# Decoder layer: who sums the norm's mean and variance in the first half, and where the residual stands

## The reference

```python
x = _layernorm(x + _L0_attn_ref(x, ...), axis=-1)
x = _layernorm(x + _L0_xattn_ref(ctx_2048, x, mask, mask, ...), axis=-1)
x = _layernorm(x + _L0_ffn_ref(x, ...), axis=-1)

def _layernorm(x, axis=-1, eps=1e-05):
    m = jnp.mean(x, axis=axis, keepdims=True)
    v = jnp.var(x, axis=axis, keepdims=True)
    return (x - m) / jnp.sqrt(v + eps)
```

## Time and profile before

| | us |
|---|---|
| median of 3 runs | 1878.28 |
| lowest, highest | 1867.21, 1881.26 |
| the profiled execution | 1870.93 |
| its span | 1869.1 |

### The profile page before, as it was taken

The page is one execution under the profiler, slowest core; times in us unless marked ns, Lnnn a source line. Parts: engine busy times, 40 slices in busy tenths (PEclk is TensorE's granted clock), DMA queues, the critical chain, the costliest instruction groups (busy, mean ns, idle before and its releaser), DMA issues. The chain is left out here.

```text
span 1869.1 us, 32453 instructions
## 1 busy us (share of the span) xinstructions
PE 1775.7 (95%) x12432; PEld 978.3 (52%) x12432; DVE 1374.0 (74%) x1466; ACT 770.5 (41%) x1208; POOL 566.8 (30%) x578
## 2 busy tenths in 40 slices
PE   7999999999999998978899999999999999999988
PEld 3665456545654564634545555455454554554543
DVE  2899999999999999957566577575675666657721
ACT  3323222222232222237657265373562744726522
POOL 3125865596559525600100302003011020030000
PEclk9999999999999999999999999999999999999999
DMA  9436346535653467556430613405205143051010
GB/s 217 128 74 136 97 124 153 130 79 137 148 123 85 118 143 184 156 147 201 103 74 2 142 46 74 113 1 130 57 14 134 40 106 81 1 137 28 13 34 23
DMA packets 295166, 183.86 MB, mean 98 GB/s; under 512 B 194015, under 2 KB 251359, under 8 KB 295038
## 3 DMA queue, kind: packets, MB, share of 16 engines
q1 hardware_dynamic: 287392, 178.50, 38.3%
q10 hardware_dynamic: 7646, 3.50, 1.0%
HBM read 94.82 MB, written 33.62 MB: 69 GB/s over the span
## 5 line engine op out<-in xcount | busy, mean ns | idle before, releaser
L1223 POOL TENSOR_TENSOR q<-q,x_hi 128x512 f16<-128x512 f32 x28 | 40.5, 1475 | 597.5 <-ACT x_hi L1571 597.5
L1251 PE MATMUL b_ff<-x2T_hi,w1T_hi 128*128 128x512 f16 x512 | 195.3, 381 | 2.3 <-DVE x2T_lo L1661 2.3
L1251 PE MATMUL b_ff<-x2T_lo,w1T_hi 128*128 128x512 f16 x512 | 195.3, 381 | 0.0
L1251 PE MATMUL b_ff<-x2T_hi,w1T_lo 128*128 128x512 f16 x512 | 195.1, 381 | 0.0
L1661 DVE TENSOR_TENSOR p_lo<-k,p_hi 128x1024 f16<-128x1024 f32 x128 | 161.3, 1260 | 37.4 <-ACT p_hi L1517 37.4
L1550 ACT ACTIVATE k<-b_st,mbias 128x512 f32<-128x512 f32 x256 | 161.9, 693 | 41.4 <-PE b_st L1318 37.9
L1711 DVE SCALAR_TENSOR_TENSOR top<-b_st,mleast,top 128x512 f16<-128x512 f32 x168 | 126.1, 751 | 51.5 <-PE b_st L1278 34.5
L825 DVE TENSOR_TENSOR prod<-q,k 128x4096 f32<-128x4096 f32 x32 | 143.0, 4469 | 20.7 <-ACT q L691 19.9
L607 PE MATMUL sm_b<-cT_hi,wsT_hi 128*128 128x256 f16 x512 | 141.1, 276 | 14.7 <-DMA cT_lo<-rows_lo 12.2
L457 POOL TENSOR_TENSOR rows_lo<-cn,rows_hi 128x512 f16<-128x512 f32 x64 | 131.4, 2061 | 61.0 <-ACT rows_hi L675 61.0
L571 PE MATMUL pj_b<-winT_hi,xT_hi 128*128 128x512 f16 x384 | 148.1, 386 | 0.9 <-DVE winT_lo L892 0.9
(11 more groups left out here) (287 smaller groups left out, 4314.1 us busy)
## 6 DMA issues: line engine op xcount, KB each, us to landing
cn<-in_ctx_dram SPq DMA_DIRECT2D x64, 256.0 KB, 3.3
k<-kT_scratch SPq DMA_DIRECT2D x24, 512.0 KB, 7.9
x<-in_x_dram SPq DMA_DIRECT2D x32, 256.0 KB, 3.1
x_scratch<-x SPq DMA_DIRECT2D x32, 256.0 KB, 2.3
q<-x_scratch SPq DMA_DIRECT2D x8, 1024.0 KB, 5.6
q<-x_scratch SPq DMA_DIRECT2D x32, 256.0 KB, 2.8
out_dram<-q SPq DMA_DIRECT2D x32, 256.0 KB, 3.3
xn<-in_x_dram SPq DMA_DIRECT2D x24, 256.0 KB, 2.9
```

What stands on the lines that cost most here:

```text
L1251: mm = pe.matmul(out, a, c, start=(start and n == 0), stop=end)
```

## The change

Three edits in `phase_a`.

- For tiles 0 to 28 (`SUMMED = 29`) VectorE stops after the residual sum. ACT gets `moments(n)`: one pass over the row that sums `-E**-1.5 * x` (into mean times `-E**-0.5`), and a second that squares `E**-0.5 * x + mv0` and sums it, which is the variance. Both write their 512 unused results into the bank `om_b[n % 2]`. They stand in ACT's order behind the copies of the projections and `normalize`, in the step in which VectorE has its residual.
- TensorE's output projection of tile n waits for `ln_mv` of tile n-2 instead of `om_used`, since ACT uses the bank until then.
- In the score steps VectorE has residual (and moments) between the products and the sums.

POOL's factors take a mean that is scaled: a product takes the place of the difference, four instructions as before.

```diff
+def layer_norm_factors_of_sums(pool, w, mv, vs, out, done, at):
+
+    pool.tensor_tensor(vs[:, :], mv[:, 1:2], w.consts[:, 1:2], ALU.add).then_inc(done, 1)
+    pool.wait_ge(done, at + 1)
+    pool.tensor_tensor(out[:, 0:1], vs[:, :], w.consts[:, 0:1], ALU.pow).then_inc(done, 1)
+    pool.wait_ge(done, at + 2)
+    pool.tensor_tensor(out[:, 2:3], mv[:, 0:1], out[:, 0:1], ALU.mult).then_inc(done, 1)
+    pool.wait_ge(done, at + 3)
+    pool.tensor_tensor(out[:, 1:2], w.consts[:, 5:6], out[:, 2:3], ALU.mult).then_inc(done, 1)
...
@@ TensorE, output_projection
                 if n >= 2:
-                    pe.wait_ge(s["om_used"], n - 1)
+                    pe.wait_ge(s["ln_mv"], n - 1)
...
@@ ScalarE
+            def moments(n):
+                i, unused = n % 3, om_b[n % 2][:, :]
+                act.wait_ge(s["om_used"], n + 1)
+                if n >= 3:
+                    act.wait_ge(s["ln_rstd"], 4 * n - 8)
+                act.activation(unused, x1[i][:, :], ACT.Identity, scale=-E ** -1.5,
+                               accum_out=mv[i][:, 0:1]).then_inc(s["ln_stats"], 1)
+                act.wait_ge(s["ln_stats"], n + 1)
+                act.activation(unused, x1[i][:, :], ACT.Square, bias=mv[i][:, 0:1], scale=E ** -0.5,
+                               accum_out=mv[i][:, 1:2]).then_inc(s["ln_mv"], 1)
...
                 for n in plan.tiles(g - 4):
                     normalize(n)
+                for n in plan.tiles(g - 3):
+                    if n < SUMMED:
+                        moments(n)
...
@@ VectorE, residual_and_moments
+                if n < SUMMED:
+                    return
                 dve.wait_ge(s["om_used"], n + 1)
+                dve.wait_ge(s["ln_mv"], n)
                 dve.bn_stats(stats[i][:, :], x1[i][:, :]).then_inc(s["ln_stats"], 1)
...
@@ VectorE, steps
                     score_products(b, t)
+                    for n in plan.tiles(g - 3):
+                        residual_and_moments(n)
                     for n in plan.quarters(g - 1):
                         stage_lo(n)
                     score_sums(b, t)
-                    for n in plan.tiles(g - 3):
-                        residual_and_moments(n)
```

## The result

| | before | after |
|---|---|---|
| median of 4 runs, us | 1877.2 | 1935.1 |
| lowest to highest, us | 1867.2 to 1881.3 | 1931.9 to 1939.6 |
| span of the profiled execution, us | 1869.1 | 1937.8 |
| mean granted clock over it | 0.987 | 0.975 |

The changed kernel is slower: ratio 1.033, 95% interval 1.030 to 1.035, some 58 us. The forecast was 1924 us within 1900 to 1948. Nearly all of it is the first half: the second begins at 819.9 us before and at 887.5 after.

The account below looks back on a forecast made before the run. TensorE and VectorE were taken to be full at once, so the effect on TensorE counts. Waits +50.4, `c1T` -7.7, `stage_lo` with its half clock -9.2, quarters -3.0, clock +20.4: +51 on 1874, given as 1924 us, range 1900 to 1948.

Parts of the forecast that it names:

- What bounds the kernel: From 60 to 810 us TensorE (718 of 750 us busy) and VectorE (707) are both full; relieving one hands on the bound.
- Where the wait falls, and how often: TensorE's output projection waits for ScalarE's moments of tile n-2 in 18 places, steps 16b+12 to 16b+17, b = 0, 1, 2.
- The price of a wait: Copy, normalize and two passes end 2.88 us behind the last p matmul's start; each wait 2.8 us, together +50.4 us.
- `c1T` never later than the moments: In these steps the new wait covers TensorE's waits for transposed attention rows, so their 7.7 us come off.
- What comes back: VectorE gets ahead of TensorE: 5.8 us for `stage_lo`, 3.4 of half clock and 3 on quarters go, -12.2 us.
- The clock: TensorE's clock halves for 3.4 us behind 12 of the 18 new idles, 1.7 us each: +20.4 us.
- The steady clock: Rival: idles of 2.6 us do not lower TensorE's clock; all else as forecast, +31, 1905 us; chance 0.15.
- The sum: 50.4 - 7.7 - 9.2 - 3.0 + 20.4 = +51 us on a base of 1874, given as 1924 us.
- Dear passes: Rival: waits for ScalarE's passes cost 3.6 us each and the clock falls each time: +75, 1950 us; chance 0.18.
- no change: Rival: TensorE's other waits take up the delay, waits 2.4 us, clock unmoved: +14, 1888 us; chance 0.08.
- faster: Rival: VectorE is the bound and the bank is free before `c1T` lands; TensorE gains 20 us: 1854 us; chance 0.07.

Follow-up runs that it names:

- E11: Kernel before, with VectorE's statistics of the first norm taken over 8 of the 512 numbers of a row: 1867.6 us, ratio 0.997.
- E2: Changed kernel, with the passes' waste for tiles 0 to 5 of each block written to an idle SBUF row buffer: 1887.8 us, ratio to before 1.008.
- E3: Changed kernel with sums by ScalarE for tiles 0 to 7 only (SUMMED = 8): 1898.4 us, ratio to before 1.012.
- E5: Kernel before, with only the residual (and its statistics) moved between products and sums in the score steps: 1874.0 us, ratio 1.001.
- E7: Kernel before, with only POOL's low halves of the attention rows moved ahead of the norm's factors: 1871.4 us, ratio 0.999.
- E1: Changed kernel, with TensorE filling its wait by 12 unused matmuls in each of 18 places: 1914.8 us, ratio to before 1.023.
- E9: E2 with POOL's low halves ahead of the norm's factors and ScalarE's moments one step later, behind the next attention row's rounding: 1880.7 us, ratio to before 1.0045.
- E10: E9 with the residual behind the sums again in the score steps: 1878.6 us, ratio to before 1.004.
- E4: Changed kernel with ScalarE's moments ahead of normalize in its step instead of behind it: 1921.9 us, ratio to before 1.025.

## Why the prediction was right, and where it was not

**What bounds the kernel: right.** E11 puts a number on it: by its quarter, an estimate, VectorE's 26 us could have brought some 7.

**Where the wait falls, and how often: right.** 18 places in steps 16b+12 to 16b+17 of blocks 0, 1 and 2. E2 takes the wait away and keeps the passes, and 47 of 62 us go; E3 keeps a third of the waits and 25 of the 62 us.

**The price of a wait: right, by parts that erred both ways.** Forecast 2.88 us behind the last p; measured 2.90. ScalarE's copy at 0.32, `normalize` at 0.50, the first pass at 1.20, as worked out from the earlier trace rows. The passes took 0.59 and 0.69 where I had 0.63 and 0.69, and the sum of each is read by an instruction of its own, 0.19 us, of which I had 0.1. I missed two things of the code. The first wait of each block is 0.7 us shorter (2.19 us instead of 2.91 from p to output projection), since no tile is normalized in that step; the last is 0.3 longer, behind a copy of v (0.60 us) in place of one of p (0.28). 12 x 2.85 + 3 x 2.14 + 3 x 3.16 = 50.1 us against 50.4. That the total came so close is partly luck, since these terms cancel. A step lasts 13.6 us and not "about 12", because the forecast of the step left out the 1.7 us of the clock, which the sum had.

**`c1T` never later than the moments: right in 17 of 18.** VectorE waits for POOL's low half ahead of its last halving, as forecast:

```profile
437.89 0.69 DVE L903 TENSOR_TENSOR ctx<-prod 128x512 f32<-128x512 f32 x1 [2.08 <-POOL rows_lo L469]
```

POOL's four factor instructions became shorter by less than forecast: together 5.7 us a tile before, 3.0 after, where I had counted 1.1. Once, in block 0, the row came 0.6 us later than the moments would have.

**What comes back: wrong.** This is the step that failed: -12.2 us forecast, of which 9.2 for `stage_lo` with its half clock and 3 for quarters; after the change `stage_lo` costs 0.6 us less and the quarters 3.6 more, so +3. The 3.6 mean little, since E5 and E7 have 5 to 6 us more on quarters at an unchanged time; but the `stage_lo` wait stands in every run, with 5.2 to 6.1 us. The reason given was that VectorE gets ahead of TensorE. It can't. Its scores of a block need all of k of that block, which TensorE projects in the steps before: VectorE now waits for them at each start of the scores, 21.3 us in three waits, where before it waited 0.7 for q. So it begins every block level with TensorE, and block 3's `stage_lo` stands behind the same softmax at the same distance as before, 22.0 us behind its start (687.41 to 709.40 before, 752.90 to 774.90 after). In E11, where nothing delays TensorE, the lead went into longer waits for `stage_hi` and `stage_v`, 18.8 us instead of 10.8, and TensorE's wait for `stage_lo` was 5.2 us all the same. A lead that is won inside a block ends at the block's first shared tile.

**The clock: the mechanism right, the size a little low.** 12 falls forecast, 14 measured; 24 us instead of 20.4, and E1 gives 20 of it back. The steady clock, the rival by the rule of the Trainium skill ("TensorE: Matmul & The Clock Gate", section on HAM oscillation), which warns only of longer gaps, fell: here the clock halved behind idles of 1.8 to 2.7 us, and the measurement decides.

**The sum.** 50.1 us of waits, 0.6 more where `c1T` ended one, 7.7 off for the old `c1T` waits, 3 for quarters and `stage_lo`, 24 for the clock: +70 us, and the two spans differ by 68.7. Against these 70 the forecast of +51 is 19 us short: the 12.2 us that did not come back, the 3 that came on top, and 3.6 of the clock. The medians differ by less, 58 to 62, so the forecast time looks better than its sum: 1935.1 is 11 us above it. (1874 + 51 is 1925, not 1924.)

**Dear passes, no change, faster:** the first fell with the 2.90 us; E1's 42 us that remain without the clock rule out the second, E11's 4 us the third.

## What to carry to other kernels

Look where a buffer is let go before counting busy time: as work the passes cost, with VectorE's relief set against them, the 7 to 9 us that stay in E9 and E10 at most, and they cost 47 us because their waste lay in a bank that the bound engine needed, behind a copy that waits for this same engine. Put work on an idle engine behind what others wait for in its order (E9), not ahead. And price an idle of the bound engine as the idle plus the half clock behind it: here 2.8 + 0.8 x 1.7 us, 0.8 being 14 of 18.

## What the runs showed of the hardware

- A pass with a sum on ScalarE is two instructions: the pass, and 0.19 us to read the sum (0.09 of it hidden by the next).
- The same pass is a little shorter when its results go into a bank of PSUM, where TensorE writes (`om_b`), than into a row buffer in SBUF (`xn`). After the change, and E2:

```profile
L727 ACT ACTIVATE om_b<-x,small 128x512 f32<-128x512 f32 x29 | 20.1, 692 | 0.9
...
L724 ACT ACTIVATE om_b<-x 128x512 f32<-128x512 f32 x29 | 17.1, 591 | 0.0
```

```profile
L730 ACT ACTIVATE xn<-x,small 128x512 f32<-128x512 f32 x23 | 16.6, 722 | 0.7
...
L727 ACT ACTIVATE xn<-x 128x512 f32<-128x512 f32 x23 | 14.2, 618 | 0.0
```

  692 against 722 ns and 591 against 618.
- TensorE's clock went from 2.4 to 1.2 GHz behind 8 of 15 idles of 2.0 us in E4, and after the change behind 10 of the 11 of 2.7 us in these places; the length of the idle alone does not decide it.
